# Two half products of the recurrence in two PSUM banks, decays of the second layer made during the tail of the first, and the second layer's state update issued earlier on VectorE

## The chip, the cores and the metric

One core of a Trainium2 chip runs the whole program in one launch. The metric is the device time of that launch in microseconds (us). The five engines (TensorE, called PE in the profile; VectorE, DVE; ScalarE, ACT; GpSimd, POOL; SyncE, SP, which here only issues DMAs) each run their own instruction list in order and meet at semaphores.

## The reference

The input is 2 sequences of 2048 tokens with 256 features. Two layers follow one another; each adds a state-space mixer and a feed-forward part to the residual. Cut to what matters here:

```python
# mixer of layer 1 (layer 0: 8 heads of 64, state 16; layer 1: 4 heads of 128, state 64)
zxbcdt = u @ in_proj_w.T                      # z, x, B, C, dt
dt  = softplus(dt_raw + dt_bias)
xBC = silu(causal_conv(xBC))                  # 3 taps in layer 0, 4 in layer 1
dA  = exp(dt * -exp(A_log))
state = state * dA + dt * x (outer) B         # for every token, per head
y     = state . C + D * x
out   = rmsnorm(y * silu(z)) * norm_w @ out_proj_w.T
# feed-forward of layer 0: an MLP and a soft decision tree
# feed-forward of layer 1: 8 experts; each takes its 1024 best-scoring tokens (top_k over all tokens)
```

## The kernel before

The 4096 tokens are cut into 8 steps of 512 tokens, and each step into 4 tiles of 128. The recurrence is done tile by tile. In a tile, y is a sum of three parts: the state carried in, times C (called inter), the part inside the tile through a masked decay matrix (intra), and D x. The carried state is then updated once per tile.

**Layer 0** is a software pipeline over the steps: step f's mixer (front) runs beside step b = f-1's MLP, tree and router (back). The order of work on each engine is written out by hand in a function `step0` on each engine. **The tail** is the last call, `step0(None, STEPS-1, None)`: only the back of the last step, and in its shadow the first projections and convolutions of layer 1. Then all engines meet at a barrier (`phase`). **The transition** is what runs between the barrier and the first tile of layer 1. In it VectorE computes softplus of dt for all 32 tiles at once (a series of some twenty small operations on 128x128), TensorE makes the running sums of the decay logs, ScalarE takes their exponents (`EX`, `dAT`), SP stores the decays to DRAM (`dA_d`) and loads them back spread over all partitions (`dAB`), and VectorE counts scores for a threshold search.

**Layer 1** is a loop over 32 tiles n, with n = 4 i + c: step i, tile c. On TensorE an iteration is `chunk1(n+1)` (z and transposed x of the next tile by `z_xt1`, then a count product, G = B C and the transposed B), `y_turned1(n-1)`, `recur1(n)`, `intra1(n)`, in c = 0 and 1 some blocks of the next step's input projection (`in_proj1`), and `project1(n-1)`. VectorE does `chunk1(n+1)` (for some tiles a round of the threshold search, `threshold`, then the decay scan and the mask), `sums1(n)` (the y sums, the state update at L2060 and the gating), the next step's convolutions in c = 0 and 1 (L1719), and `mixed1(n-1)`. ScalarE does silu of z, the x rows and D x for n+1 (L1190 to L1197), the transposed y, and `inter_read(n)` (L1317). A threshold search of 15 rounds is spread over the tiles of the first five steps: one in every tile but those with c = 1.

**The experts** follow: 16 units of 512 gathered tokens.

**PSUM use that matters.** bank[0] holds in turn z and inter, bank[1] xt (transposed x) and the new part of the state. In both layers the recurrence (`recur`, `recur1`) issues three blocks: the first half of inter (contracting 64 partitions, 0 to 63), the two halves of the state product (128 partitions, 64 columns each), and the second half of inter (partitions 64 to 127). Both halves of inter write bank[0], and the second is issued only when the first has ended:

```python
mm(p[:, 0:2 * P], cb[0:64, cols(c)], S1[0:64, :]).then_inc(s1.half.sem, 1)
... # two state products into bank[1], columns 0 to 255
s1.half.wait_ge(pe, i, c + 1)
filled1(mm(p[:, 2 * P:4 * P], ub[64:P, 4, cols(c)], S1[64:P, :]), "inter")
```

A bank is given back by its readers: xt of tile n+1 is written when the state update of tile n-1 is done (`open1`). The G product of tile n+1 waits for the mask of tile n, and `y_turned1(n)` for the gated y of tile n.

Of the kernel before, what the change touches and what calls it, by code (L numbers as in the profile page):

```python
# [144 lines left out]
def program(nc, d, out):  # L145
    ctx = ExitStack()
    with ctx:
# [125 lines left out]
        DT, WEND, ADT, DA = (lp1[:, 384 + P * k:384 + P * (k + 1)] for k in range(4))  # L273
        leaf1 = leaf[:, :, :].rearrange("p c n -> p (c n)")
        SCT, G8, Q8 = leaf1[:, 0:256], leaf1[:, 256:384], leaf1[:, 384:392]
        dAT = E[:, 0, 512:512 + P]
# [105 lines left out]
        for L in LAYERS[0:1]:  # L382
# [48 lines left out]
        s1.e_in, s1.e_out, s1.a, s1.cum_full, s1.ex, s1.w_end, s1.dA, s1.dAT_full = (counted(x, 1) for x in (  # L431
            s0.e_in, s0.e_out, s0.a, s0.cum_full, s0.ex, s0.w_end, s0.r, s0.v))
# [102 lines left out]
        TILES1 = CH * STEPS  # L535

# [62 lines left out]
        def _(sp):  # L599
# [137 lines left out]
            store_back(STEPS - 2)  # L737
            store_back(STEPS - 1)
            for s in (rows_stored, nT_stored, sc_stored, x1_stored):
                sp.wait_ge(s.sem, 16 * STEPS)  # L740
# [8 lines left out]
            def load_decays(i, half):  # L749
                s1.E.wait_ge(sp, i - 1, 2 * half + 2)  # L750
                sp.dma_start(dAB[half], dA_d[2 * i + half].partition_broadcast(P)).then_inc(s1.dA_loaded[half].sem, 16)

# [8 lines left out]
            s1.dAT.wait_ge(sp, 0, 2)  # L761
            sp.dma_start(dA_d.rearrange("m (r t) -> (m r) t", t=P), dAT).then_inc(s1.dA_stored.sem, 16)
            s1.dA_stored.wait_ge(sp, 0, 16)
            load_decays(0, 0)
            load_decays(0, 1)
# [3 lines left out]
            sp.dma_start(b2f[:, :], d["e_b2"]).then_inc(eb_loaded.sem, 16)  # L769
            for i in range(STEPS):  # L770
                if i + 1 < STEPS:
                    load_decays(i + 1, 0)
# [32 lines left out]
        def _(pool):  # L805
# [133 lines left out]

            rstd(0)  # L940
# [9 lines left out]
            step0(None, STEPS - 1, None)  # L950
            pool.drain().then_inc(phase, 1)
            pool.wait_ge(phase, 5)

            def xrows1(i, c):

                q, n = c % 2, CH * i + c
                hd = slice(NH1 * n, NH1 * (n + 1))
                s1.xsb.wait_ge(pool, i, c + 1)
                s1.w_end.wait_ge(pool, 0, 1)
                front1(pool, "state", n - 2)  # L960
                x3 = Xsb[:, q, :].rearrange("p (h e) -> p h e", h=NH1)
                g.tensor_tensor(Xs[:, q, :].rearrange("p (h e) -> p h e", h=NH1), x3,  # L962
                                WEND[:, hd].unsqueeze(2).to_broadcast([P, NH1, P]), ALU.mult).then_inc(s1.xs.sem, 1)
# [23 lines left out]
            def gather(u, first=0, last=4):  # L987

                q = u % 2
                idx_ready.wait_ge(pool, 0, u // 2 + 1)  # L990
                xt_full.wait_ge(pool, u - 2, KD)
# [7 lines left out]
            xrows1(0, 0)  # L999
# [40 lines left out]
        def _(act):  # L1040
# [159 lines left out]

            def step0(f, b, n):
# [23 lines left out]
                if f is None:  # L1225
                    raw1(0, 4)
# [56 lines left out]
                if b is not None:  # L1283
                    smx_sig.wait_ge(act, b, 1)
                    a.activation(sx[:, 1, :, :], sx[:, 0, :, :], ACT.Exp).then_inc(sme_sig.sem, 1)

# [16 lines left out]
            def dt_diagonals(n):  # L1303
                s1.E.wait_ge(act, 0, n - 1)
                for k in range(NH1):
                    ins = a.activation(DG[n % 2][:, P * k:P * (k + 1)], ident[:, :], ACT.Copy,
                                       scale=DT[:, NH1 * n + k:NH1 * n + k + 1])
                ins.then_inc(s1.dg.sem, 1)

            def inter_read(i, c):  # L1310
                q, n = c % 2, CH * i + c
                p = front1(act, "inter", n)
# [3 lines left out]
                for k in range(NH1):  # L1316
                    ins = a.activation(yb[:, q, P * k:P * (k + 1)], p[:, P * k:P * (k + 1)], ACT.Copy,  # L1317
# [33 lines left out]
            s1.e_in.wait_ge(act, 0, 1)  # L1351
            a.activation(L1T[1], L1T[1], ACT.Exp).then_inc(s1.e_out.sem, 1)
            s1.a.wait_ge(act, 0, 1)
            a.activation(DA, ADT, ACT.Exp).then_inc(s1.dA.sem, 1)
            s1.cum_full.wait_ge(act, 0, 1)
            a.activation(EX, SEG[:, 0:3 * P].rearrange("p (j n) -> p j n", j=3), ACT.Exp).then_inc(s1.ex.sem, 1)
            s1.dAT_full.wait_ge(act, 0, 1)
            a.activation(dAT[:, 1:P], INTRA[:, 1:P], ACT.Copy).then_inc(s1.dAT.sem, 1)
            dt_diagonals(0)
            dt_diagonals(1)  # L1360
            for n in range(TILES1):
# [18 lines left out]
                elif following and c == 2:  # L1380
                    for j in range(2, 5):
                        silu1(i + 1, j)
                elif n + 3 == TILES1:
# [55 lines left out]
        def _(dve):  # L1439
# [228 lines left out]
            def sums(L, s, i, c, ch):  # L1668
                q, nh, hp, n = c % 2, L.heads, L.hp, 64
                ex3 = s.ex_buf[:, :, c * nh:(c + 1) * nh]  # L1670
                p = front_wait(dve, L, s, i, f"inter{c}")
# [7 lines left out]
                v.tensor_tensor(yb[:, q, :].rearrange("p (h e) -> p h e", h=nh),  # L1679
                                p[:, :].rearrange("p (h e) -> p h e", h=nh),  # L1680
                                ex3[:, 0, :].unsqueeze(2).to_broadcast([P, nh, hp]),
                                ALU.mult).then_inc(s.t1.sem, 1)
# [48 lines left out]

# [989 lines left out]
```

## Time and profile before

| quantity | value |
|---|---|
| median of 3 runs | 1498.16 us (1497.09 to 1503.91) |
| the profiled execution: its own time | 1497.89 us |
| its span (first to last instruction) | 1496.1 us |
| PE / DVE / ACT / POOL busy | 95% / 70% / 52% / 33% |
| mean granted PE clock | 0.975 of full speed |
| layer 0 and tail / transition and layer 1 / experts, about | 722 / 363 / 411 us |

The 1.8 us between the span and the time of the execution lie before and after the instructions. Busy shares are means over stages that differ, so each stage is read by itself.

### The profile page before, as it was taken

To read this page: it belongs to the slowest core of one execution; us is meant where nothing else is said; L and a number is where in the kernel's file an instruction comes from. 1 tells how busy PE (TensorE), PEld (TensorE's weight loads), DVE (VectorE), ACT (ScalarE), POOL (GpSimd) and SP (SyncE) were. 2 spreads that over 40 slices of the span, in tenths; PEclk is the share of its full clock that TensorE was granted. 3 is DMA by queue.
4 is the path that set the end of the run, shared out by engine and by line. 5 is a ranking of instruction groups with operands and counts; after the bars stand their busy time and mean duration, and the time that the engine had idled before them with its cause. 6 is when DMAs were issued, how large, how long until landed. Compare 5 with 4: busy or idle time off the path is not lost.

```text
span 1496.1 us, 23276 instructions
## 1 busy us (share of the span) xinstructions
PE 1423.5 (95%) x7571; PEld 1067.6 (71%) x7571; DVE 1046.7 (70%) x2438; ACT 773.4 (52%) x1608; POOL 489.9 (33%) x599
## 2 busy tenths in 40 slices
PE   6899999999999999999599999999999999999996
PEld 4567768686867768687355655565688898989895
DVE  7978686868778686835698887889765555555542
ACT  4362533526262533524377765877665555555552
POOL 1443243342424243331111221221324543454343
PEclk9999999999999999999699998999999999999998
DMA  7120201203030201210411221221134333433322
GB/s 238 46 71 15 100 29 58 70 11 116 0 113 14 99 28 44 83 44 14 167 41 39 71 67 40 71 71 54 33 83 107 84 84 72 104 84 85 72 48 29
DMA packets 71849, 100.94 MB, mean 67 GB/s; under 512 B 13000, under 2 KB 58192, under 8 KB 71760
## 3 DMA queue, kind: packets, MB, share of 16 engines
q1 hardware_dynamic: 59472, 82.77, 16.9%
q0 software_dynamic: 12288, 17.05, 6.7%
q8 instruction: 48, 0.79, 0.2%
q14 instruction: 41, 0.34, 0.1%
HBM read 74.30 MB, written 25.49 MB: 67 GB/s over the span
## 4 chain that ended last, share of the span: by engine, by line
PE 77%; DVE 13%; ACT 4%; issue 3%; POOL 1%; DMA 1%; SPq 0%; DVEq 0%; ACTq 0%; POOLq 0%
PE bank L2200 70%; DVE am L1719 3%; DVE u L1719 2%; PE bank L2313 1%; PE bank L2600 1%; DVE E L2030 1%; PE bank L2277 1%; PE bank L2339 1%; PE bank L2538 1%; DVE hits L1922 1%; POOL out L1020 1%; PE bank L2396 1%; ACT am L1142 1%; DVE yb L2040 1%; ACT tg L1103 1%
## 5 line engine op out<-in xcount | busy, mean ns | idle before, releaser
L2159 DVE TENSOR_TENSOR aml<-m0big,amh 128x512 fp32r<-128x512 f32 x128 | 88.1, 689 | 175.3 <-ACT amh L1408 168.3
L1020 POOL DMA_INDIRECT out<-EW,IDX x64 | 103.6, 1620 | 220.3 <-DVE EW L2154 205.7
L1403 ACT ACTIVATE m0big<-bank,eb 128x512 f32<-128x512 f32 x128 | 87.9, 687 | 161.5 <-PE bank L2200 139.2
L2200 PE MATMUL bank<-w2h,amh 128*128 128x256 f32 x512 | 147.9, 289 | 0.0
L2200 PE MATMUL bank<-w2h,aml 128*128 128x256 f32 x512 | 144.7, 283 | 0.0
L2200 PE MATMUL bank<-w2l,amh 128*128 128x256 f32 x512 | 144.6, 282 | 0.0
L2200 PE MATMUL bank<-EW,am 128*128 128x256 f32 x512 | 115.8, 379 | 0.0
L1142 ACT ACTIVATE am<-bank,b 128x512 f32<-128x512 f32 x64 | 43.5, 681 | 135.7 <-PE bank L2200 134.9
L962 POOL TENSOR_TENSOR Xs<-Xsb,lp 128x512 f32<-128x512 f32 x32 | 43.4, 1356 | 194.7 <-ACT Xsb L1194 185.4
L2200 PEld LDWEIGHTS bank<-EW,am 128*128 128x128 f32 x512 | 97.2, 190 | 13.5 <-ACT am L1142 0.3
L2200 PEld LDWEIGHTS bank<-w2h,amh 128*128 128x128 f32 x512 | 97.6, 191 | 8.3 <-issue 5.8
L2200 PE MATMUL bank<-xTh,w1h 128*128 128x512 f32 x256 | 102.1, 399 | 0.0
L2200 PE MATMUL bank<-xTl,w1h 128*128 128x512 f32 x256 | 100.7, 394 | 0.0
L2200 PE MATMUL bank<-xTh,w1l 128*128 128x512 f32 x256 | 99.7, 390 | 0.0
L2200 PEld LDWEIGHTS bank<-w2l,amh 128*128 128x128 f32 x512 | 97.8, 191 | 2.2
L2200 PEld LDWEIGHTS bank<-w2h,aml 128*128 128x128 f32 x512 | 97.7, 191 | 0.0
L1408 ACT ACTIVATE amh<-m0big 128x512 fp32r<-128x512 f32 x128 | 80.9, 632 | 4.1
L994 POOL DMA_INDIRECT xg<-rows_d,IDX x64 | 67.6, 1057 | 19.1 <-issue 19.1
L865 POOL TENSOR_TENSOR xb<-x,xp 128x256 f32<-128x256 f32 x32 | 22.2, 726 | 146.7 <-ACT u L1075 139.2
L2200 PE MATMUL bank<-m0big,hT 128*128 128x512 f32 x128 | 61.3, 602 | 4.6 <-DVE yb L1679 2.7
L2200 PE MATMUL bank<-EW,yT 128*128 128x256 f32 x256 | 63.3, 392 | 0.0
L2200 PE MATMUL bank<-m0big,yT 128*128 128x256 f32 x256 | 61.9, 385 | 0.7 <-ACT yT L1128 0.7
(349 smaller groups left out, 3652.0 us busy)
## 6 DMA issues: line engine op xcount, KB each, us to landing
EW<-in_e_w SPq DMA_DIRECT2D x16, 1024.0 KB, 6.1
dA0b<-dA_d SPq DMA_DIRECT2D x16, 512.0 KB, 3.8
E<-dA_d SPq DMA_DIRECT2D x16, 512.0 KB, 5.3
m0big<-dA_d SPq DMA_DIRECT2D x16, 512.0 KB, 4.9
xin<-in_L_attn_x SPq DMA_DIRECT2D x8, 512.0 KB
xp<-in_L_attn_x SPq DMA_DIRECT2D x8, 512.0 KB, 3.8
rows_d<-xo SPq DMA_DIRECT2D x8, 512.0 KB, 3.0
x_d<-xb SPq DMA_DIRECT2D x8, 512.0 KB
```

What stands on the lines that cost most here:

```text
L865: g.tensor_tensor(xb[:, c, :], x2[:, c, :], xp[:, c, :], ALU.add).then_inc(xb_sig.sem, 1)
L962: g.tensor_tensor(Xs[:, q, :].rearrange("p (h e) -> p h e", h=NH1), x3, WEND[:, hd].unsqueeze(2).to_broadcast([P, NH1, P]), ALU.mult).then ...
L994: g.indirect_dma_start(out=xg[:, q, c, :], out_offset=None, in_=rows_d, in_offset=bass.IndirectOffsetOnAxis(ap=IDX[:, 4 * u + c:4 * u + c ...
L1020: g.indirect_dma_start(out=out_rows, out_offset=bass.IndirectOffsetOnAxis(ap=IDX[:, 4 * u + c:4 * u + c + 1], axis=0), in_=ye[:, q, c, :], ...
L1103: a.activation(tg[:, c, :], p[:, (c % 2) * LEAVES:(c % 2 + 1) * LEAVES], ACT.Tanh, scale=gs[:, 1, c:c + 1]).then_inc(tg_sig.sem, 1)
L1142: a.activation(am[:, k, :], p[:, :], ACT.Silu, bias=b1[:, k:k + 1]).then_inc(am_sig.sem, 1)
L1403: a.activation(am2[:, j % 2, :], bank[j % 2][:, :], ACT.Gelu, bias=eb1[:, u // 2, j:j + 1]).then_inc(gelu_sig.sem, 1)
L1408: a.activation(amh[:, j % 4, :], am2[:, j % 2, :], ACT.Copy).then_inc(am_high.sem, 1)
L1719: ins = v.scalar_tensor_tensor(out=ub[:, blk, :], in0=xbuf[:, blk, k:k + T], scalar=w[:, blk, k:k + 1], in1=ub[:, blk, :], op0=ALU.mult, o ...
L1922: ins = v.tensor_scalar(hits1, SCT, cand[:, j:j + 1].bitcast(fp32), 0.0, ALU.is_ge, ALU.add, accum_out=cnt[:, j:j + 1])
L2159: v.tensor_tensor(aml[:, j % 4, :], am2[:, j % 2, :], amh[:, j % 4, :], ALU.subtract).then_inc(am_low.sem, 1)
L2200: return t.matmul(out_, lhsT, rhs, start=first, stop=last)
```

## The change

Three things are changed.

1. In both layers the second half of inter is written into bank[1], columns 256 to 511, which the state product leaves free. It is issued directly behind the first half and waits for nothing more; both banks are opened before the first half. Readers (VectorE `sums` in layer 0, ScalarE `inter_read` in layer 1) read two halves out of two banks: VectorE in two instructions instead of one, ScalarE in the same four. The second half is read once the state product is done too.
2. dt, decay logs, exponents and decay rows of layer 1 are made in two parts. Part 0 (tiles 0 to 27, all that is known when the tail starts) is done inside the tail, on all engines, with its store and the first two loads of decays; so are the z, x, G, mask and scaled x rows of tile 0 and z and x of tile 1. Part 1 (tiles 28 to 31) is made inside the loop at n = 15, 18 and 19. The clearing of the state moves in front of the tail. The barrier no longer waits for the store of the scores; those who read them do. Round 0 of the threshold search moves from tile 0 to tile 1.
3. In layer 1 the state update becomes `state1`, apart from the y sums. For c = 1 and 2 it stands ahead of the next tile's `chunk1` (threshold round, scan, mask), for c = 0 and 3 behind it and ahead of the y sums.

```diff
 TensorE, layer 0 (recur) and layer 1 (recur1):
                 p = open_front(pe, L, s, i, f"inter{c}")
+                r = open_front(pe, L, s, i, f"state{c}")
                 s.S.wait_ge(pe, i, c + 1)
+                s.c2.wait_ge(pe, i, 1)
                 mm(p[:, 0:2 * P], s.Ct_buf[:, cols(c)], S1[0:64, :]).then_inc(s.half.sem, 1)
-                r = open_front(pe, L, s, i, f"state{c}")
+                filled(mm(r[:, 2 * P:4 * P], C2[:, cols(c)], S1[64:P, :]), s, L, f"inter{c}")
                 s.bs.wait_ge(pe, i, c + 1)
                 s.xs.wait_ge(pe, i, c + 1)
                 mm(r[0:64, 0:2 * P], Bs[:, q, :], Xs[:, q, 0:2 * P])
                 filled(mm(r[64:P, 0:2 * P], Bs[:, q, :], Xs[:, q, 2 * P:4 * P]), s, L, f"state{c}")
-                s.half.wait_ge(pe, i, c + 1)
-                s.c2.wait_ge(pe, i, 1)
-                filled(mm(p[:, 2 * P:4 * P], C2[:, cols(c)], S1[64:P, :]), s, L, f"inter{c}")
...
                 p = open1("inter", n)
+                r = open1("state", n)
                 mm(p[:, 0:2 * P], cb[0:64, cols(c)], S1[0:64, :]).then_inc(s1.half.sem, 1)
+                filled1(mm(r[:, 2 * P:4 * P], ub[64:P, 4, cols(c)], S1[64:P, :]), "inter")
                 s1.xs.wait_ge(pe, i, c + 1)
-                r = open1("state", n)
...
 TensorE, tail (step0 with f is None) and transition:
+                if f is None:
+                    z_xt1(0, 0)
                 if b is not None:
                     down(b, 1, 0, KD + HB)
+                if f is None:
+                    decay_sums1(0)
...
-                else:
-                    z_xt1(0, 0)
                 (the nT transposes)
+                else:
+                    chunk1(0, 0)
                 (the router products)
...
+            z_xt1(0, 1)
             pe.drain().then_inc(phase, 1)
...
 ScalarE, tail:
                 if f is None:
+                    dt_exp1(0)
                     raw1(0, 4)
...
                     chunk1(0, 0)
+                    decay_exps1(0)
+                    dt_diagonals(0)
+                    dt_diagonals(1)
...
 VectorE, tail and loop of layer 1:
+            v.memset(SS[:, :], 0.0).then_inc(prepped, 1)
+            for rows in dAT:
+                v.memset(rows[:, 0:1], 0.0).then_inc(s1.dAT.sem, 1)
+            dt_begin1(0)
             step0(None, None, STEPS - 1)
...
                     for j in range(5):
                         conv1(0, j)
+                    dt_steps1(0)
...
                     (the four next-layer norms, xo)
+                    if f is None:
+                        s1.g_full.wait_ge(dve, 0, 1)
+                        masked1(0, 0)
...
+            def state1(i, c):
+                n = CH * i + c
                 s1.t1.wait_ge(dve, i, c + 1)
+                if n + 1 == TILES1:
+                    return
                 p = front1(dve, "state", n)
                 s1.S.wait_ge(dve, i, c)
...
             for n in range(TILES1):
                 i, c = divmod(n, CH)
                 following = i + 1 < STEPS
+                if c in (1, 2):
+                    state1(i, c)
                 if n + 1 < TILES1:
                     chunk1(*divmod(n + 1, CH))
+                if c in (0, 3):
+                    state1(i, c)
                 sums1(i, c)
...
+                elif n == 15:
+                    dt_steps1(1)
+                elif n == 19:
+                    dt_ends1(1)
...
 SP:
+            store_decays1(0)
+            load_decays(0, 0)
+            load_decays(0, 1)
             store_back(STEPS - 1)
-            for s in (rows_stored, nT_stored, sc_stored, x1_stored):
+            for s in (rows_stored, nT_stored, x1_stored):
```

## Rows read from the trace of the kernel before

**Rows 1.** The page: the chain that ended last, shares by engine

```profile
PE 77%; DVE 13%; ACT 4%; issue 3%; POOL 1%; DMA 1%; SPq 0%; DVEq 0%; ACTq 0%; POOLq 0%
```

**Rows 2.** Stretches: length, busy PE, PEld, DVE, ACT, POOL, PE clock, DMA share, GB/s

```profile
34.00:604.00 570.00, 559.53 (x2812) 413.68 (x2810) 433.21 (x982) 243.25 (x490) 205.11 (x300) 0.99 0.18 58
...
722.00:746.00 24.00, 11.33 (x39) 6.73 (x40) 18.37 (x58) 7.92 (x22) 5.13 (x8) 0.56 0.50 177
746.00:972.00 226.00, 214.46 (x911) 132.04 (x910) 191.68 (x422) 163.17 (x425) 46.45 (x60) 0.95 0.17 56
972.00:1085.00 113.00, 108.89 (x513) 68.29 (x512) 97.40 (x195) 81.53 (x217) 29.69 (x39) 0.97 0.16 52
```

**Rows 3.** Timeline of PE: one recurrence in layer 0, then a long product

```profile
455.71 0.70 PE L2200 MATMUL bank<-S,Ct 64*128 64x256 f32 x2
456.34 0.65 PE L2200 MATMUL bank<-Xs,Bs 128*64 128x256 f32 x4
456.92 0.70 PE L2200 MATMUL bank<-S,Ct 64*128 64x256 f32 x2
457.55 2.00 PE L2200 MATMUL bank<-Xdt,E 128*128 128x64 f32 x16
...
479.50 3.62 PE L2200 MATMUL bank<-EW,am 128*128 128x256 f32 x16
```

**Rows 4.** Timeline of DVE in layer 0: read of inter, state update

```profile
458.18 0.68 DVE L1679 TENSOR_TENSOR yb<-bank,ex 128x512 f32<-128x512 f32 x1
...
461.28 0.41 DVE L1694 TENSOR_TENSOR S<-S,bank 128x256 f32<-128x256 f32 x1
```

**Rows 5.** Timeline of PE in the tail: z of tile 0, transposes of xo

```profile
711.42 1.88 PE L2200 MATMUL bank<-EW,hT 128*128 128x512 f32 x4
...
713.88 1.28 PE L2467 MATMUL bank<-ident,xo 128*128 128x128 f32 x8
```

**Rows 6.** Timeline of DVE in the tail: idle before the first norm

```profile
698.75 0.42 DVE L1788 TENSOR_TENSOR xb<-bank,xb 128x256 f32<-128x256 f32 x1 [6.37 <-PE bank L2200]
```

**Rows 7.** The chain that ended last, across the barrier and the transition

```profile
719.98 1.75 DMA rows_d<-SC
...
722.03 0.48 DVE S L1875
...
723.04 0.28 DVE dA0b L1886
...
734.63 0.90 DVE cand L1915
...
737.14 1.31 PE bank L2200 x4
...
749.53 0.76 DVE am L1719
```

**Rows 8.** Timeline of PE: its waits in layer 1, and products after one

```profile
776.21 0.63 PE L2396 MATMUL bank<-ident,am 128*128 128x128 f32 x4 [3.47 <-DVE S L2060]
822.25 0.63 PE L2396 MATMUL bank<-ident,u 128*128 128x128 f32 x4 [2.30 <-DVE S L2060]
864.61 0.63 PE L2396 MATMUL bank<-ident,am 128*128 128x128 f32 x4 [1.78 <-DVE S L2060]
...
869.79 2.07 PE L2200 MATMUL bank<-Xsb,E 128*128 128x128 f32 x8
...
911.18 1.08 PE L2396 MATMUL bank<-ident,u 128*128 128x128 f32 x4 [2.84 <-DVE S L2060]
```

**Rows 9.** Timeline of DVE, layer 1, step 2: gating, threshold, gating

```profile
836.81 0.69 DVE L2047 TENSOR_TENSOR yb<-yb,zs 128x512 f32<-128x512 f32 x1
...
845.56 0.16 DVE L1932 TENSOR_SCALAR_CACHE_REDUCE hits<-bank 128x3 bf16<-128x3 f32 x1
...
864.38 0.68 DVE L2047 TENSOR_TENSOR yb<-yb,zs 128x512 f32<-128x512 f32 x1
```

**Rows 10.** Timeline of ACT in the same step: projection copy, inter read

```profile
842.43 0.59 ACT L1168 ACTIVATE xbuf<-bank 128x512 f32<-128x512 f32 x1
...
846.92 1.14 ACT L1317 ACTIVATE yb<-bank,lp 128x128 f32<-128x128 f32 x4
```

More of the change, by code:

```diff
@@ L535, in program @@
         TILES1 = CH * STEPS
+        SPLIT = TILES - CH
+        PARTS = (slice(0, NH1 * SPLIT), slice(NH1 * SPLIT, P))
+        ROUNDS = {1: 0}
+        ROUNDS.update((n, 3 * (n // CH) + n % CH - (n % CH > 0)) for n in range(2, 5 * CH) if n % CH != 1)
         def front1(eng, kind, n):
@@ L760, in _ @@
             load_x1(1)
[L761 to L765, printed above, removed]
             load_w1(0)
@@ L1301, in _ @@
             act.wait_ge(phase, 5)
[L1303 to L1308, printed above, removed]
             def inter_read(i, c):
                 q, n = c % 2, CH * i + c
-                p = front1(act, "inter", n)
+                s1.half.wait_ge(act, i, c + 1)
+                s1.ex.wait_ge(act, 0, 1 + (n >= SPLIT))
                 s1.yo_full.wait_ge(act, i, 2 * (c - 2) + 1)
@@ L1316, in inter_read @@
                 for k in range(NH1):
-                    ins = a.activation(yb[:, q, P * k:P * (k + 1)], p[:, P * k:P * (k + 1)], ACT.Copy,
+                    if k == 2:
+                        front1(act, "inter", n)
+                        front1(act, "state", n)
+                    ins = a.activation(yb[:, q, P * k:P * (k + 1)], bank[k // 2][:, P * k:P * (k + 1)], ACT.Copy,
                                        scale=EX[:, 0, NH1 * n + k:NH1 * n + k + 1])
@@ L1670, in sums @@
                 ex3 = s.ex_buf[:, :, c * nh:(c + 1) * nh]
-                p = front_wait(dve, L, s, i, f"inter{c}")
+                p = bank[front_use(L, f"inter{c}")[0]], bank[front_use(L, f"state{c}")[0]]
+                s.half.wait_ge(dve, i, c + 1)
                 if c >= 2:
@@ L1678, in sums @@
                     s.yo_full.wait_ge(dve, i - 1, 2 * (c + 2) + 1)
[L1679 to L1682, printed above, removed]
+                for half in range(2):
+                    sl, hs = slice(2 * P * half, 2 * P * (half + 1)), slice(nh // 2 * half, nh // 2 * (half + 1))
+                    if half:
+                        front_wait(dve, L, s, i, f"inter{c}")
+                        front_wait(dve, L, s, i, f"state{c}")
+                    ins = v.tensor_tensor(yb[:, q, sl].rearrange("p (h e) -> p h e", h=nh // 2),
+                                          p[half][:, sl].rearrange("p (h e) -> p h e", h=nh // 2),
+                                          ex3[:, 0, hs].unsqueeze(2).to_broadcast([P, nh // 2, hp]), ALU.mult)
+                ins.then_inc(s.t1.sem, 1)
                 s.S.wait_ge(dve, i, c + 1)
@@ new lines, in dt_begin1 @@
+            def dt_begin1(part):
+                cs, ts = PARTS[part], slice((0, SPLIT)[part], (SPLIT, TILES)[part])
+                x, e = L1T[0][:, cs], L1T[1][:, cs]
+                dtr_sig.wait_ge(dve, STEPS - 1 + part, 0)
+                op(v.tensor_tensor(x.rearrange("p (t h) -> p t h", h=NH1), RT[:, ts, :],
+                                   W[1]["dtb"][:, :].unsqueeze(1).to_broadcast([P, ts.stop - ts.start, NH1]),
+                                   ALU.add))
+                v.scalar_tensor_tensor(out=e, in0=x, scalar=-1.0, in1=x, op0=ALU.mult, op1=ALU.min
+                                       ).then_inc(s1.e_in.sem, 1)
@@ new lines, in dt_ends1 @@
+            def dt_ends1(part):
+                cs, ts = PARTS[part], slice((0, SPLIT)[part], (SPLIT, TILES)[part])
+                s1.ex.wait_ge(dve, 0, part + 1)
+                v.tensor_tensor(WEND[:, cs], DT[:, cs], EX[:, 1, cs], ALU.mult).then_inc(s1.w_end.sem, 1)
+                for half in range(2):
+                    rows = slice(64 * half, 64 * (half + 1))
+                    op(v.tensor_copy(EXS[rows, 2 * ts.start:2 * ts.stop].rearrange("p (t k) -> p t k", k=2),
+                                     EX[rows, 2, cs].rearrange("p (t h) -> p t h", h=NH1)
+                                     [:, :, 2 * half:2 * half + 2]))
@@ L1814, in step0 @@
                         residual(c)
+                        if f is None and c == 2:
+                            dt_ends1(0)
                 if isinstance(f, int) and f == 0:
```

229 lines of the change are left out of this document (124 added, 105 removed).

## The prediction

> **What bounds the kernel now.** First the page's chain: 77% of it is PE, 13% DVE [rows 1]. Then the busy times by stretch [rows 2]. In layer 0 PE is busy 559.5 of 570 us: what PE is spared there is gained, as long as DVE (433 of 570) keeps up. In the transition PE is busy 11.3 of 24 us at a mean clock of 0.56, so it does little and much of that at the lower level (1.2 of 2.4 GHz). In layer 1's first 226 us PE is busy 214 at a mean clock of 0.95, DVE 192: two engines close to each other. The timeline of PE shows what lies between: it waits for the state update L2060 once per step, 3.47, 2.30, 1.78 and 2.84 us, and products after such a wait can take twice as long (the transposes behind the last wait 1.08 us, behind the others 0.63; after the third the eight intra products took 2.07) [rows 8]. The experts (411 us) are not touched.
>
> **Part 1, inter in two banks.** From starts in the timeline [rows 3]: first half 455.71 to 456.34, 0.63; state products 0.58; second half 0.63; 1.84 in all. The state block shows that two products in different column halves of the array run side by side: four instructions take 0.58 us where the two of one half of inter take 0.63. No row shows this for two row halves, which the new order puts back to back. Bounds: they overlap wholly and the second is free, 0.63 saved per tile; or not at all, and only the refilling of the array is spared, at most 0.2 (0.63 less twice the 0.226 per instruction of the long product, 3.62/16), at least nothing. I take full overlap, by the nearest row, the column pair. The Trainium skill (TensorEngine Tiling, Key Properties) says that tiles operate independently and can execute loads and matmuls in parallel; no run here has shown it for rows yet.
>
> What it is worth in layer 0: 0.63 x 4 = 2.5 us per step. Tile 0 gives less: both banks are now opened ahead of the first half, which must wait for the x rows of the next tile (about 0.35 lost). DVE reads the halves by two instructions: a 512-wide one takes 0.68, a 256-wide one 0.41 [rows 4], but they overlap in issue, so 0.1 more per tile. DVE is nearly full between tiles 0 and 2; by its order it gates y of tile 2 just as PE would turn it 2 us earlier. So 2.1 per step; six to seven steps are bound by PE: 14 us (bounds 8 and 17). If there is no overlap: 0.2 x 4 x 7 at most, less DVE's 0.1, so 0 to 5, I take 2.
>
> **Part 2, tail and transition.** Removed from the transition: the wait for the store of the scores, 1.75, clearing the state 0.48, some twenty small operations on DVE from 723.04 on, and the sums, exponents, store and load behind them [rows 7]. Added ahead of the tail on DVE: the clearing and dt's first steps, 0.5 + 0.3 + 0.3 = about 1.2, on the path (DVE's scaled rows are what PE turns next). dt's series (some 6 us) lies on DVE between the convolutions and the first norm, where it idles 6.37 us [rows 6]: hidden by that, 6 us if the cover were gone. On PE in the tail z and x of tile 0 stood at 711.42 to 713.88, just ahead of the transposes of xo [rows 5], and covered the norm before them. Now they lie in front of two long products, so that cover is gone: 2.3, and the sums add 0.8. ScalarE is freed in turn: its tile 0 work no longer stands ahead of the nT copies, and the exponent table is loaded already, together some 2.5 back. DVE's first scan and mask (2.0) stand ahead of its router copies and cost about 2. With the store's 1.75 no longer awaited, the barrier comes at 721.9 + 1.2 + 2.3 + 0.8 - 2.5 + 2 - 1.8 = about 724, 2 later. SP's store of decays and two loads stand ahead of the last rows' store, but are over long before those rows exist.
>
> Behind the barrier DVE has a cast, two small operations and the scores' copy (about 1.6), and the first count (734.63 to 737.14, 2.5 [rows 7]), so 728 to 729.5; then PE's count product, G and recurrence at half clock; DVE a threshold round (2.1), scan and mask 2.0, update and y sums (2.4). The gating of tile 0 then ends near 736 instead of 749, and the first convolution, which waits for the first projection, starts near 737.5 instead of 749.53 [rows 7]. Gain of tail and transition together 12 us, bounds 9 and 15. Part 1 of the decays costs DVE 3.5 at n = 15 and ScalarE two table loads at n = 18; DVE is in the bound there, 2 us.
>
> **Part 3, the state update.** In before, PE waits each step at xt of the next step's tile 0 for S of tile 2, updated only after DVE's y sums [rows 8]. Take step 2: gating of tile 0 at 836.81, threshold of tile 2's chunk at 845.56, gating of tile 2 at 864.38, PE released at 864.61 [rows 8, 9]. The update moves 4.5 us of work ahead, so S of tile 2 is in time. But what is late next? In c = 1 `state1` stands ahead of the threshold and waits for ScalarE's inter read. That starts at 846.92 and ends at 848.06, and it isn't held by PE's second half: ScalarE works without a gap from its copy at 842.43 [rows 10]. DVE is at that point at 845.56: it stalls 2.5 us, in each of seven steps, and all behind it shifts: the mask of tile 3, on which PE's next G waits, ended about 862.5 (the gating at 864.38 less the update and two sums, 1.9) and will end near 865.5 (2.5 and the update's 0.5 later), while PE is there at 862.7 (864.61 less its wait of 1.78 less 0.6, plus 0.44 for xt). The gating of tile 2, on which `y_turned1` waits, ends at 867.5 instead of 865.0; PE turned it about 1.1 after its release, 865.7. So PE's wait of 1.8 becomes two of together 5, and the step's point of release comes 1.8 later. After it PE gains 1.2 (two recurrences) and loses some 3.5 if the clock falls. From release to release the steps take 46.0, 42.4 and 46.6 [rows 8]: the one without a low stretch is about 4 shorter. The granted clock fell after the waits of 3.47, 1.78 and 2.84 and not after 2.30. A step with rounds would take 42.8 at full clock and 46.2 with one low stretch; the steps up to 972 take 226/5 = 45 now [rows 2]. With a low stretch in four of five: 4 x 45.5 + 44.5 = 226.5 against 223.5 for the same stretch without the transition's end: 3 us lost (bounds: 10 gained at full clock, 9 lost), the 2 of decay part 1 included. In the last three steps, without rounds, PE is busy 109 of 113 us [rows 2]: 12 tiles x 0.6 = 7, of which the one-hot operations on DVE and the same stall leave about 3 (bounds 0 and 7).
>
> **Sum.** -14 - 12 + 3 - 3 = -26. The profiled execution took 1497.9 (span 1496.1 and 1.8 around it), 0.3 from the median of 1498.2: 1472.
>
> **Rivals.**
> - The clock stays full in layer 1 (chance 0.20): as where a wait of 2.30 left it. Then part 3 with part 1 gives 10 in the rounds' steps and 6 in the last, layer 0 17: 17 + 12 + 10 + 6 = 45, 1453. Against it: the waits I expect are longer than those that lowered it.
> - Row halves don't overlap (0.15): layer 0 gives 2, the late steps nothing, transition 12, rounds' steps -3 to +1: about -12, 1486. For it: no row shows row halves together.
> - Half an overlap (0.08): if instructions start strictly in order, and each product is two, B's first can only join A's second; the pair takes 0.63 + 0.23, 0.4 per tile saved. Layer 0 then gives 9 and the sum is 21: 1477. The row speaks against it, the column pair takes no longer than one half. This is what the Trainium skill's page "TensorE: Matmul & The Clock Gate" (The mechanism) would make of it: matmuls are strict first in, first out in start and end.
> - Slower (0.04): DVE's stall in `state1` feeds on itself: PE's two waits close after one another double the low stretch of each of the five rounds' steps, and the later PE is, the later t1, S and the mask. One stretch costs 3.6 to 4.2 (46.0 and 46.6 against 42.4 [rows 8]); two in each of five steps where I counted one in four are 6 x 4 = 24 more. With the stall of c = 1 met again in c = 2 (2.5 in seven steps) it is 41 against the gains of 26: 1513. It decides from 6.7 per step on (33.5/5), since 26 + 7.5 must be eaten. The longest wait, 3.47, lowered it for one stretch only, which speaks against it.
> - Nearly no change (0.05): no overlap, and a low stretch in every step: 1492 to 1500.
>
> The likeliest, in its own range 1463 to 1481, has the remaining 0.48. Faster by over 0.5% (7.5 us, about what a measurement of this kernel can tell from no change) covers all but the last two: 0.91; same 0.05; slower 0.04. Range: from the full clock case, 1452, to the case without overlap and a little over, 1489.
>
> **What would show it.** Right: in PE's timeline both halves of inter begin together and the block takes 1.2, and a middle step of layer 0 is 2 us shorter; the barrier near 724 and the first convolution near 737; in layer 1 no wait for L2060, but DVE idle some 2.5 before the update in c = 1, released by L1317, and PE's waits at G and at the turned y, released by DVE's mask and gating. Wrong: a second half that starts 0.4 or more after the first; a PE that waits in layer 0 for DVE's y read or gating more than it gained; an update in c = 1 without idle time (then ScalarE is faster than I read it and layer 1 gains 10 or more); or a barrier after 727.

## The result, and the profile after

The changed kernel takes 1485.33 us (median of four runs, 1482.22 to 1487.28), the kernel before beside it 1501.04 (1497.09 to 1504.00): ratio 0.9895, interval 0.9861 to 0.9930. A second set of runs of the same two kernels gave 1485.07 against 1503.47, ratio 0.9885 (0.9856 to 0.9914). So it is faster by 16 to 18 us where 26 were forecast. The profiled execution took 1485.9 (span 1484.1). Executions of one kernel differ by more than that: the kernel before took 1497.09 to 1516.75 over all its runs, and its profiled one (1497.89) is among the quickest, so the spans below differ by 12.0 us where the medians differ by 16 to 18.

First the stretches of the changed kernel, cut at the events that the table below names (columns as in [rows 2]):

```profile
31.30:595.70 564.40, 547.56 (x2813) 409.81 (x2813) 436.02 (x1012) 244.96 (x495) 203.55 (x300) 0.98 0.18 60
722.00:746.00 24.00, 21.75 (x84) 13.05 (x85) 21.05 (x53) 15.19 (x37) 3.06 (x5) 0.86 0.39 135
731.50:959.50 228.00, 205.33 (x908) 129.27 (x907) 194.86 (x437) 163.31 (x426) 44.46 (x60) 0.92 0.16 54
959.50:1070.40 110.90, 100.70 (x492) 63.81 (x491) 96.33 (x190) 78.66 (x212) 29.85 (x36) 0.95 0.16 52
```

And two stretches of the kernel before, cut at the same events of layer 1:

```profile
748.40:971.80 223.40, 211.86 (x902) 130.61 (x901) 189.11 (x418) 162.24 (x422) 46.45 (x60) 0.95 0.17 55
971.80:1082.10 110.30, 106.85 (x498) 66.39 (x496) 94.97 (x192) 79.53 (x212) 28.55 (x36) 0.97 0.16 52
```

In layer 1 PE has 6.5 and 6 us less to do than before, and both stretches are no shorter. What PE is spared went into waits and a lower mean clock (0.92 for 0.95, 0.95 for 0.97). The 24 us of the old transition are full of work now, PE is busy 21.75 of them where it was 11.33.

The table has the same cuts for the profiled execution of every kernel that ran: from the start to the scaling of the router's weights on DVE (L1447 before, L1475 after), with which the tail begins; to the barrier (POOL's iota behind it); to the gating of layer 1's tile 0; to that of tile 20 (the five steps with rounds); to that of tile 31; to the end. Columns in us; the last but one is the span.

| kernel | layer 0 | tail | transition | 5 steps | last | experts | span | ratio |
|---|---|---|---|---|---|---|---|---|
| before | 675.0 | 46.9 | 26.5 | 223.3 | 110.3 | 414.0 | 1496.1 | 1 |
| changed | 664.9 | 54.3 | 12.3 | 228.0 | 110.9 | 413.7 | 1484.1 | 0.9895 |
| changed, again | 661.8 | 54.1 | 12.3 | 227.8 | 111.0 | 413.9 | 1480.8 | 0.9885 |
| update first in c=2 only | 665.2 | 54.3 | 12.3 | 220.9 | 109.6 | 413.9 | 1476.2 | 0.9831 |
| update behind the chunk | 664.0 | 53.9 | 12.3 | 220.5 | 105.8 | 413.5 | 1469.9 | 0.9803 |
| update behind the sums | 667.3 | 54.4 | 12.1 | 222.2 | 103.3 | 414.4 | 1473.7 | 0.9792 |
| z of tile 1 behind the barrier | 662.0 | 52.5 | 11.7 | 227.4 | 112.0 | 413.8 | 1479.3 | 0.9879 |
| z of tile 1 as cover | 665.3 | 50.3 | 12.3 | 228.7 | 111.0 | 414.0 | 1481.5 | 0.9867 |
| halves in turn | 701.7 | 53.0 | 12.4 | 239.0 | 115.7 | 414.4 | 1536.2 | 1.0167 |
| before + banks, layer 0 | 662.0 | 47.0 | 26.2 | 234.5 | 111.8 | 414.2 | 1495.6 | 0.9922 |
| before + banks, both layers | 665.9 | 46.9 | 25.8 | 220.4 | 104.8 | 413.4 | 1477.2 | 0.9842 |
| update behind + z as cover | 665.6 | 50.2 | 12.3 | 222.7 | 105.2 | 413.6 | 1469.6 | 0.9778 |

The first column varies by 5.5 us among kernels whose layer 0 is the same (661.8 to 667.3), and the clock of the start goes with it. The mean granted clock of the first 110 us is 0.97 in four rows: before (675.0), changed again (661.8), z of tile 1 behind the barrier (662.0) and banks in layer 0 (662.0). In the other rows with the new layer 0 it is 0.91 to 0.95, and they have 664.0 to 667.3; halves in turn stands apart. So at the same clock there, layer 0 is 13 us shorter than before.

A step of layer 0, from one scaling of S to the next, in the changed kernel and in the kernel before:

```profile
349.69 0.35 DVE L1644 TENSOR_SCALAR S<-S,flags 128x256 f32<-128x256 f32 x1
431.92 0.35 DVE L1644 TENSOR_SCALAR S<-S,flags 128x256 f32<-128x256 f32 x1
...
352.84 0.35 DVE L1616 TENSOR_SCALAR S<-S,flags 128x256 f32<-128x256 f32 x1
436.83 0.35 DVE L1616 TENSOR_SCALAR S<-S,flags 128x256 f32<-128x256 f32 x1
```

Now the places that the prediction names. PE's timeline of the changed kernel, the recurrence in layer 0 that answers to [rows 3], and one in layer 1, where the records are apart because the tiles have other names:

```profile
450.87 0.70 PE L2267 MATMUL bank<-S,Ct 64*128 64x256 f32 x4
451.50 0.65 PE L2267 MATMUL bank<-Xs,Bs 128*64 128x256 f32 x4
452.09 2.00 PE L2267 MATMUL bank<-Xdt,E 128*128 128x64 f32 x16
...
748.83 0.48 PE L2267 MATMUL bank<-S,Ct 64*128 64x256 f32 x1
748.83 0.48 PE L2267 MATMUL bank<-S,u 64*128 64x256 f32 x1
749.14 0.38 PE L2267 MATMUL bank<-S,Ct 64*128 64x256 f32 x1
749.15 0.38 PE L2267 MATMUL bank<-S,u 64*128 64x256 f32 x1
749.46 0.65 PE L2267 MATMUL bank<-Xs,Bs 128*64 128x256 f32 x4
```

All four instructions of both halves take 0.63 (450.87 to 451.50), what one half took before; the block to the intra products is 1.22 instead of 1.84. The halves begin in the same 10 ns.

The end of the tail on PE, in the same kernel (to be held against [rows 5]):

```profile
707.80 0.63 PE L2561 MATMUL bank<-ident,xo 128*128 128x128 f32 x4 [2.36 <-DVE xo L1917]
709.17 1.09 PE L2561 MATMUL bank<-ident,xo 128*128 128x128 f32 x4 [0.74 <-DVE xo L1917]
...
711.02 3.59 PE L2267 MATMUL bank<-wr,nT 128*128 128x12 f32 x16
714.45 3.76 PE L2267 MATMUL bank<-EW,hT 128*128 128x512 f32 x4
718.01 1.00 PE L2466 MATMUL bank<-ident,u 128*128 128x128 f32 x4
```

and DVE's timeline there:

```profile
716.51 0.19 DVE L1945 TENSOR_TENSOR SC<-sx,sm 128x32 f32<-128x32 f32 x1
719.22 0.06 DVE L1977 MEMSET thrf<- 128x2 f32 x1 [2.52 <-SPq L760]
```

PE waits 2.36 for xo, the cover that went away, and from 709.17 to the barrier its work takes twice the usual time (granted clock 0.5 from 709 to 719): the four instructions of z (`EW,hT`) 3.76 against 1.88 at 711.42 before [rows 5]. DVE has the scores at 716.7; the barrier opens at 719.2, when PE is through with tile 1.

Layer 1, step 2, DVE's timeline around the updates in c = 1 and c = 2:

```profile
820.83 0.69 DVE L2130 TENSOR_TENSOR yb<-yb,zs 128x512 f32<-128x512 f32 x1
...
829.37 0.06 DVE L1762 MEMSET xbuf<- 128x3 f32 x1
831.79 0.61 DVE L2117 SCALAR_TENSOR_TENSOR S<-S,dA0b,bank 128x128 f32<-128x128 f32 x2 [2.36 <-ACT yb L1353]
...
837.85 0.69 DVE L2130 TENSOR_TENSOR yb<-yb,zs 128x512 f32<-128x512 f32 x1
...
848.35 0.69 DVE L1777 TENSOR_TENSOR E<-E,bank 128x512 f32<-128x512 f32 x1
...
850.47 0.69 DVE L2130 TENSOR_TENSOR yb<-yb,zs 128x512 f32<-128x512 f32 x1
```

and PE's eight intra products of tile 1, then its waits behind the updates:

```profile
830.30 1.16 PE L2267 MATMUL bank<-Xsb,E 128*128 128x128 f32 x8
...
849.14 0.56 PE L2267 MATMUL bank<-cnt,leaf 128*128 128x3 f32 x2 [3.01 <-DVE E L1777]
849.63 0.79 PE L2267 MATMUL bank<-am 64*128 64x128 f32 x2
...
851.21 1.11 PE L2622 MATMUL bank<-ident,yb 128*128 128x128 f32 x4 [0.68 <-DVE yb L2130]
...
854.68 2.08 PE L2267 MATMUL bank<-Xsb,E 128*128 128x128 f32 x8
```

DVE stands still for 2.36 us in front of the update of c = 1, until ScalarE has read inter. The tile's gating comes 17.0 after the last one (820.83 to 837.85), the mask of tile 3 at 848.35 to 849.04, and PE, which wants it, waits 3.01; its intra products then take 2.08 for eight where they took 1.16 at 830.30. Step 2 is the worst of the steps: DVE's wait in front of the update of c = 1 is 0.19, 1.56, 2.36, 1.50 and 0.77 us in the five steps with rounds (together 6.4) and 1.49, none and 0.49 in the last three.

The sums over PE's waits in layer 1 (window 735 to 1085; total us, times, longest):

```profile
PE bank L2267 <- DVE E L1777: 14.7, 6, 3.3
PE bank L2622 <- DVE yb L2130: 11.3, 8, 3.4
PE bank L2267 <- ACT Xsb L1207: 6.6, 16, 1.9
PE bank L2466 <- DVE S L2117: 0.2, 1, 0.2
```

Before, the same view of the same window had one line of weight for the steps:

```profile
PE bank L2396 <- DVE S L2060: 14.0, 6, 3.5
PE bank L2200 <- DVE hits L1922: 3.6, 1, 3.6
PE bank L2538 <- DVE yb L2047: 1.6, 2, 1.0
```

The wait for S is gone, as the edit intends: 14.0 us are now 0.2. In its place stand 14.7 for the mask, 11.3 for the gating and 6.6 for the x rows.

### The profile page after: what moved, and what is told of

Its sections match the earlier page's. It is cut to its first block, busy times and chain, and to the rows that moved or that the text cites. A ratio compares the mean times of both kernels' runs of the same rounds, so it can differ in the third digit from the quotient of the medians.

```text
span 1484.1 us, 23444 instructions
## 1 busy us (share of the span) xinstructions
PE 1398.2 (94%) x7578; PEld 1061.1 (71%) x7578; DVE 1053.4 (71%) x2493; ACT 773.4 (52%) x1612; POOL 488.9 (33%) x599
## 4 chain that ended last, share of the span: by engine, by line
PE 78%; DVE 10%; ACT 6%; issue 4%; PEldq 0%; POOL 0%; DMA 0%; SPq 0%; DVEq 0%; PEld 0%; ACTq 0%
PE bank L2267 72%; DVE am L1753 1%; DVE E L1773 1%; PE bank L2379 1%; DVE u L1753 1%; PE bank L2680 1%; PE bank L2405 1%; PE bank L2344 1%; DVE yb L2130 1%; DVE yb L2127 1%; DVE yb L2125 1%; ACT am L1155 1%; DVE hits L2000 1%; ACT tg L1116 1%; ACT Xsb L1207 1%
## 5 line engine op out<-in xcount | busy, mean ns | idle before, releaser
L2267 PEld LDWEIGHTS bank<-EW,am 128*128 128x128 f32 x512 | 97.2, 190 | 13.5 <-ACT am L1155 0.3
L960 POOL TENSOR_TENSOR Xs<-Xsb,lp 128x512 f32<-128x512 f32 x32 | 37.9, 1184 | 198.9 <-ACT Xsb L1207 198.9
L1008 POOL DMA_INDIRECT xg<-rows_d,IDX x64 | 67.9, 1061 | 19.1 <-issue 19.1
```

The source lines that it names most:

```text
L1008: g.indirect_dma_start(out=xg[:, q, c, :], out_offset=None, in_=rows_d, in_offset=bass.IndirectOffsetOnAxis(ap=IDX[:, 4 * u + c:4 * u + c ...
L2267: return t.matmul(out_, lhsT, rhs, start=first, stop=last)
```

## Experiments

Diffs are against the changed kernel unless "before" is said. The first run is the changed kernel itself again, for a second comparison and profile.

> The changed kernel once more, beside the three edits of it that run on the same chip. Both theories: 0.988 to 0.992 of the time before. It is the measure for the next three.

Measured 1485.07, ratio 0.9885. Its steps in layer 1 (44.0, 45.2, 46.4, 46.6, 45.7) are those of the first profile to 0.1 (44.1, 45.2, 46.4, 46.6, 45.7): the pattern of waits and low stretches is the same in both profiled executions.

**The update first in c = 2 alone.** It takes away the stall of c = 1 and keeps the order that brings S of tile 2 in time.

```
-                if c in (1, 2):
+                if c == 2:
                     state1(i, c)
                 if n + 1 < TILES1:
                     chunk1(*divmod(n + 1, CH))
-                if c in (0, 3):
+                if c != 2:
                     state1(i, c)
```

> The changed kernel with the state update ahead of the next tile's work in c = 2 alone; in c = 1 it stands behind it, ahead of the y sums. My theory (VectorE's wait for ScalarE's inter read in c = 1, 1.5 to 2.4 us per step, shifts the step's mask and gating and with them PE): the wait is gone, gating of tile 2 comes 1.5 to 2.4 earlier in each of the steps with rounds, 5 x 2 = 10 us faster than the changed kernel, more if the clock no longer drops. Rival (PE's point of release is set by something else, the early update in c = 1 is what lets PE in): same or slower by up to 5 us, with a wait of PE for the update of tile 1.

Measured 1476.80 (1474.51 to 1482.33), ratio 0.9831 (0.9800 to 0.9862): 8.3 less than the changed kernel beside it. The five steps take 220.9 for 227.8, at a mean clock of 0.94 for 0.92. PE's waits for the mask fall from 14.7 us to 4.8, in three places; those for the gating are 12.2. So the stall in c = 1 costs 7 to 8 us.

**The update behind the chunk in every c**, ahead of the sums only.

```
-                if c in (1, 2):
-                    state1(i, c)
                 if n + 1 < TILES1:
                     chunk1(*divmod(n + 1, CH))
-                if c in (0, 3):
-                    state1(i, c)
+                state1(i, c)
                 sums1(i, c)
```

> The changed kernel with the state update behind the next tile's work in all c, but still ahead of the y sums. My theory: the wait in c = 1 is gone, but in c = 2 the update comes 4 us later than in e2, so PE waits for it at the transposed x of the next step: its release at about the time of the mask (within 0.6), since both end together; within 3 us of e2, and faster than the changed kernel by 5 to 10 us. Rival (the update ahead of the rounds is worth the wait of 2 to 3 us per step that it removed from PE): slower than the changed kernel by 5 to 15 us.

Measured 1472.04 (1470.58 to 1477.67), ratio 0.9803 (0.9773 to 0.9832): 13 less than the changed kernel, more than the 5 to 10 forecast, and 4.8 less than with c = 2 first (those two intervals overlap). PE's waits of this kernel in layer 1 (same window):

```profile
PE bank L2463 <- DVE S L2117: 12.1, 6, 3.2
PE bank L2619 <- DVE yb L2130: 5.7, 7, 1.2
```

and the two of step 2 in its timeline:

```profile
844.62 0.63 PE L2463 MATMUL bank<-ident,am 128*128 128x128 f32 x4 [1.59 <-DVE S L2117]
846.64 1.08 PE L2619 MATMUL bank<-ident,yb 128*128 128x128 f32 x4 [0.81 <-DVE yb L2130]
```

The wait for S is back with 12.1 us, and yet the kernel is faster. Where it stands is cheap: the sum of waits is 23.4 us (with 5.6 for the x rows) against 32.8, the gating of tile 1 comes 15.1 after tile 0's instead of 17.0, and step 2 takes 42.6 instead of 46.4. The third part of the change took away one wait and made others that cost more.

**z of tile 1 behind the barrier.** `z_xt1(0, 1)` moves from before the barrier to behind the transposes of the scores.

> The changed kernel with z and x of tile 1 made on PE behind the barrier, after the transposes of the scores, instead of ahead of it. Theory (PE's products at the low clock, 714.5 to 719.0, set the barrier, and PE idles 4.3 us behind it): the barrier comes 2.3 us earlier, the products fit in the idle time; first convolution 2 to 2.5 us earlier, 2 us faster. Rival (the barrier is set by the store of the rows or another engine): the barrier moves by less than 0.5 and the time stays.

Measured 1484.45 (1481.03 to 1487.23), ratio 0.9879 (0.9851 to 0.9907), not told apart from the changed kernel. The tail is 1.7 shorter where 2.3 were forecast, and the first convolution comes 1.0 to 1.3 earlier from the tail's start (66.2 against 67.2 and 67.5), where 2 to 2.5 were; the last steps are 1 longer. Behind the barrier z is still made at the low clock:

```profile
714.90 3.62 PE L2267 MATMUL bank<-EW,hT 128*128 128x512 f32 x4
```

It takes nearly as long as ahead of the barrier (3.76). DVE now has the scores at 713.8 and the barrier opens at 714.4, so by this timeline DVE's way is the next limit; no run tests that.

**The two halves of inter in turn.** In both layers PE waits, between the halves, for its own first one; the banks stay.

```
+                s.half.wait_ge(pe, i, c + 1)
                 filled(mm(r[:, 2 * P:4 * P], C2[:, cols(c)], S1[64:P, :]), s, L, f"inter{c}")
```

> The changed kernel, but the second half of inter waits until the first has ended, in both layers; it keeps its own bank. Theory (the halves run side by side and that is what layer 0 gained): the pair takes 1.1 to 1.3 us instead of 0.63, a middle step of layer 0 is some 1.8 us longer, as long as before, and the time is 10 to 14 us above the changed kernel, ratio 0.995 to 0.999. Rival (the gain of layer 0 came from one mode change less or from earlier reads): time within 4 us of the changed kernel.

Measured 1531.81 (1520.69 to 1537.91), ratio 1.0167 (1.0116 to 1.0218). PE's timeline of it in layer 0, and in layer 1:

```profile
479.50 1.45 PE L2267 MATMUL bank<-S,Ct 64*128 64x256 f32 x4
480.88 0.65 PE L2267 MATMUL bank<-Xs,Bs 128*64 128x256 f32 x4
...
857.69 0.70 PE L2267 MATMUL bank<-S,Ct 64*128 64x256 f32 x2
858.45 0.70 PE L2267 MATMUL bank<-S,u 64*128 64x256 f32 x2
```

The pair takes 1.38 (479.50 to 480.88) where it took 0.63. Of this, 0.63 is the second half laid bare and 0.12 the wait itself (the second starts 0.76 after the first). That is 0.75 in each of 32 tiles, 24 us in layer 0; the first column of the table grew by 37 (701.7 against 664.5, the mean of the eight changed kernels with the same layer 0). The rest goes with a lower clock. The last full step of layer 0 keeps the full clock and takes 84.5 against 81.6, 2.9 more, about four times 0.75; the four steps before it have a low stretch each (mean clock 0.96) and take 88.4 to 88.9 against 82.2 to 82.8. This profiled execution is the slowest of the six (1537.91, clock 0.961); the quickest two took 1520.7 at 0.974, still 35 more than the changed kernel. By the medians it is 46 above the changed kernel, by the ratios 42, where 10 to 14 were forecast: neither range was met. The overlap is shown by it; its price in this form is larger than what the banks gain, since the wait sits with nothing queued to cover it.

**Banks alone, on the kernel before.** First in layer 0 only (the diff's lines of `recur` and of DVE's first y product), then in both layers.

> The kernel before with the two banks in layer 0 alone, nothing else. Theory: a middle step of layer 0 is 1.8 us shorter than 84.0, layer 0 as a whole 8 to 11 us, and nothing is lost later: 1492 beside 1501, ratio 0.992 to 0.995. Rival (a faster layer 0 only moves a wait to its end): ratio above 0.997.

Measured 1493.89, ratio 0.9922 (0.9892 to 0.9952), as forecast, but not "nothing lost later". The twelve runs spread from 1482.72 (clock 0.976) to 1499.15 (0.966); the profiled one, 1497.36, is one of the slower. Layer 0 gains 13 in the profiled execution, but layer 1, which has not a line changed, takes 11 longer in its five steps (234.5 for 223.3) at a mean clock of 0.90 instead of 0.95. One profile does not say whether this belongs to the kernel or to that execution.

> The kernel before with the two banks for the inter halves in both layers, nothing else of the change: the decays stay behind the barrier, the update stays where it was. My steps: layer 0 gives 9 to 12 us as where it was done in layer 0 alone, layer 1 little more, since the wait that ends before the recurrence's mask products there is for VectorE and not for TensorE's own products: time 1487 to 1494, ratio 0.988 to 0.993, and the stretch from the barrier to the first convolution stays at about 27.5. Rival (TensorE is the bound in layer 1 too, so each of its 32 tiles gives 0.6): layer 1 gives a further 15 or more, time 1473 to 1480, ratio 0.979 to 0.984.

Measured 1481.24 (1475.88 to 1482.59), ratio 0.9842 (0.9805 to 0.9878): neither range was met, it lies between them. Layer 1 alone gives 8.4 (2.9 in the five steps, 5.5 in the last ones) of 20 that 32 times 0.63 would make. The wait for S took 5 of the missing 12: it is 19.1 us in this kernel, 14.0 before. The mean clock of the five steps is lower too (0.93 for 0.95). The longest line of that wait, in PE's timeline:

```profile
766.82 0.63 PE L2404 MATMUL bank<-ident,am 128*128 128x128 f32 x4 [4.49 <-DVE S L2069]
```

Two banks alone, a fraction of the change, are thus at least as fast as the whole of it: their six times (1475.88 to 1482.59) lie below the ten of the changed kernel (1482.22 to 1488.80) but for 0.4 us, though the intervals of the ratios overlap (0.9842 and 0.9885).

**The third part undone whole** (the update behind the sums, as before), the other two parts kept:

```
+                s1.t1.wait_ge(dve, i, c + 1)      (ahead of the sums)
...
+                state1(i, c)                      (behind the sums, ahead of the gating)
```

> The changed kernel with the third part undone whole: the update stands where it stood before, between the y sums and the gating. It tells the update's place ahead of the y sums from its place ahead of the threshold rounds. By the run with the update behind the rounds and ahead of the sums (13 us faster than the changed kernel): if being ahead of the sums is worth something, PE's wait for the update grows by the two sums, 1.2 us per step, and this run is 5 to 10 us slower than that one, 0.984 to 0.987; if only the gating counts, since PE waits for the gated y right behind it, it is the same within 3 us, 0.979 to 0.982.

Measured 1472.94 (1469.35 to 1475.38), ratio 0.9792 (0.9754 to 0.9831), the same as with the update behind the chunk, as the second reading forecast. Its waits in the same window:

```profile
PE bank L2464 <- DVE S L2117: 18.8, 6, 4.5
PE bank L2620 <- DVE yb L2132: 1.3, 2, 1.1
```

So the place ahead of the sums is worth nothing that these runs can tell: it turns 7 us of waits for S into 4 for the gating and 3 for the x rows, and the time stays. The third part as written costs 12 us by the medians, 14 by the ratios.

**z of tile 1 as cover for xo.**

```
                 if n is not None:
                     dt_of(L, s, n)
                     in_proj(L, s, n, 0)
                 elif f is not None:
                     in_proj1(0, 0)
+                else:
+                    z_xt1(0, 1)
...
-            z_xt1(0, 1)
             pe.drain().then_inc(phase, 1)
```

> The changed kernel with z and x of tile 1 made between the last long product of the tail and the transposes of xo, where PE now waits 2.36 us for VectorE's norm. Theory (the tail lost its cover: the wait there brings the clock down, and 4.5 us of products at the low clock then set the barrier): no wait above 1 us there, the stretch from the last layer 0 weights scaling on VectorE to the barrier 3 to 4.5 us shorter than 54.2, time 3 to 4 us below the changed kernel. Rival (the tail is held by VectorE's scan, mask and router copies): the barrier moves less than 1.5 us.

Measured 1483.18 (1478.69 to 1489.13), ratio 0.9867 (0.9826 to 0.9908). PE's timeline there:

```profile
705.69 1.88 PE L2267 MATMUL bank<-EW,hT 128*128 128x512 f32 x4
707.41 0.60 PE L2466 MATMUL bank<-ident,u 128*128 128x128 f32 x4
708.22 0.63 PE L2563 MATMUL bank<-ident,xo 128*128 128x128 f32 x4 [0.21 <-DVE xo L1917]
...
710.62 1.96 PE L2267 MATMUL bank<-wr,nT 128*128 128x12 f32 x16
```

The wait of 2.36 is 0.21, z takes 1.88 for 3.76 and the router's products 1.96 for 3.59. The tail is 50.3 for 54.2: the lost cover and the low clock behind it cost 4 of the 7.4 that the tail grew by. The tail is as forecast, the time is not: 2 us less than the changed kernel by the medians, and not told apart from it (ratio 0.9867 against 0.9885, intervals overlapping).

**The two mends together**: update behind the chunk, and z as cover.

> The changed kernel with the update of the second layer behind the recurrence's second chunk in every c (as in the run where that alone was moved) and the product z and the transpose xt of tile 1 between the last long product of the tail and the transposes of xo. Theory (the two edits are in different stretches, so they add up): the stretch from the scaling of the router's weights to the barrier takes 50 to 51 us in place of 54, the barrier to the first convolution about 13, and the steps of the second layer run as with the update moved alone: time 1468 to 1472, ratio to the kernel before 0.976 to 0.980. Rival (what the tail gains is taken back by the first step of the second layer, as it was where tile 1's work was moved alone and the time was unclear): 1472 to 1476, ratio 0.980 to 0.984.

Measured 1471.21 (1468.62 to 1473.48), ratio 0.9778 (0.9743 to 0.9813), 14 to 16 us faster than the change as written and within the range forecast. Against the update behind alone the tail gained 3.7 and the five steps gave 2.2 back, and the spans are equal (1469.6, 1469.9): of the two mends only the first is shown to be worth something in the time.

## Why the prediction was right, and where its sizes were off

Its mechanisms were found in their places, but for the end of the tail; the sum was 8 to 10 us too good. The 1485.3 measured lies inside the stated range (1452 to 1489) but outside that of the likeliest case (1463 to 1481). Taken alone it fits best the rival without overlap (1486), which the timeline rules out, so the time by itself confirms nothing: the rows and the runs do. Against the spans of the two profiled executions (1496.1 less 1484.1, 12.0), the 26 forecast miss 14, and the table says where: layer 0 3.9, tail 5.4, the five steps 1.7, the last steps 3.6.

- **Overlap of the row halves**: right, 0.63 saved per pair. The Trainium skill, TensorEngine Tiling (Array Packing), Key Properties, says that different tiles of the array can work in parallel; this case's trace agrees, for row halves too (both start at 748.83). The rival of the half overlap, a pair of 0.86 and a block of 1.44, is refuted by the block's 1.22. It followed the Trainium skill, TensorE: Matmul & The Clock Gate, The mechanism, which says that products start and end strictly in the order of the program. The records also list the second half's first instruction (748.83) ahead of the first half's second (749.14); whether the order of issue is product by product was not tried.
- **Layer 0, −14**: right mechanism, and nearly the size. By the starts of S's scaling a loop step went from 83.98 to 82.2, 1.8 and not 2.1. Four times 0.63 less 0.61, the wait of tile 0 for the x rows in the trace (taken as 0.35), is 1.9. Where the clock of the first 110 us was the same as before (0.97), layer 0 gained 13. The 10.1 of the pair of profiles compared here is smaller because the changed kernel met a clock of 0.92 there.
- **Tail, +2**: the term that was most mis-sized. The barrier came 7.4 later from the tail's start (46.9 to 54.3). Layer 0's gain left out, as the forecast of 724 had it, that is 729, and the first convolution comes near 742 instead of 737.5: the sign of being wrong that the prediction named, a barrier after 727, was met. The lost cover was counted with 2.3 and was 2.36, but not what follows it: the products behind the wait ran at half clock, the router's and z of tile 1, and z, put last ahead of the barrier, set it. "ScalarE's 2.5 back" and the store's 1.75 came off a path that no longer ended the tail. The step that failed is that the tail was costed as a sum on DVE and PE at full clock, though [rows 8] had shown what a wait of 1.78 or of 2.84 can do to the products behind it. z as cover gives back 4 of the 5.4.
- **Transition**: right. From barrier to first convolution 13.5 were worked out and 13.1 measured (719.23 to 732.36), 27.6 before.
- **Layer 1, five steps, +3**: right in kind, +4.7, and the nearness of the sum is in part luck. DVE's stall in c = 1 was forecast with 2.5 in every step, from step 2 alone; it was 2.36 in step 2 and 6.4 in all five, half of the 12.5. The waits at the mask and at the turned y are there in step 2 with 3.01 and 0.68 (together 5 were forecast). The low stretch came in five steps of five and not in four. The sum also used 45.5 and 44.5 per step where the lines before it had worked out 46.2 and 42.8; those give 227.6, 4 lost. That the stall costs, and is not only seen, is shown by moving the update: −7 in these steps with c = 2 alone first.
- **Last three steps, −3**: mis-sized, +0.6. The same waits go on there without the rounds; the runs that undo the third part piece by piece have 110.9, 109.6 without the early update in c = 1, 105.8 without that in c = 2 either, and 103.3 with the update behind the sums. So the early update in c = 2 costs half of it (3.8). The 103.3 are 7.6 less than changed and 7.0 less than before, which is just the upper bound named (12 tiles times 0.6). I took DVE's one-hot work for part of the loss; it is not.
- **What the forecast missed as a whole**: it priced the third part as nearly even (the wait for S removed against two others). The banks alone give 1481.24 (ratio 0.9842, 24 us), with the decays 1472.94 (0.9792), so the decays are worth some 7 to 8 more where 12 were forecast (the intervals of these two overlap); the third part takes back 12 to 14 us of it. Its own working (a longer stall, two waits for one) spoke for that, and the comparison to make was with the two parts alone and not with the kernel before.

Of the rivals, full clock in layer 1 did not come (mean clock 0.92, lower than before); "slower" did not either: the stall did not feed on itself, each of the five steps has one low stretch. What stays open: why the kernel with banks in layer 0 alone runs layer 1's unchanged steps in 234.5 us at 0.90, and why the clock of the first 110 us differs between kernels with the same layer 0. Both are differences in the granted clock; what tips it wasn't tried.

## What to carry to other kernels

A wait removed is worth what the next one leaves of it: before an operation is moved ahead on a busy engine, write down what its new neighbours wait for, and prefer the place where its operand is already there. When a product that covers a wait is moved, look for another to take its place: an uncovered wait of 2.4 us and the products behind it, which ran at half clock, cost the tail 4 (the whole time did not show it clearly). And cost each part of a change against the kernel with the other parts in, since the first two here were worth some 30 us and hid a third that lost 12 to 14.

## What the runs showed of the chip

Products in the two row halves of the array, into two banks, run side by side: four instructions of 256 columns in 0.63 us, 1.38 with a wait between the halves. That wait costs 0.12 beyond what it lays bare.

The same unchanged code took 223 us in one kernel's profiled execution and 235 in another's, at a granted clock of 0.95 and 0.90, while the two profiles of the changed kernel agree within 0.2 on such a stretch (228.0 and 227.8). The first 110 us differ in the same way (clock 0.91 to 0.97), which moves layer 0 by up to 5.5. Whether the edit of an early stage brought this about in the late one, or only that execution, isn't shown. Stages are to be compared together with their granted clock and with the whole time.
